# Four dense graph layers, fp32, 64 graphs: row sums by SBUF transfers, products two slots behind the units, and last roots on ScalarE

## The chip, the cores and the metric

One core of a Trainium2 chip runs the whole program. TensorE, VectorE, ScalarE and GpSimd each take their instructions in program order from their own queue, SyncE issues all transfers, and semaphores tie the five together. The metric is the device time of one execution in microseconds (us).

## The reference

There are 64 graphs of 128 nodes with 128 features, all fp32. Each graph goes through four layers, each with a residual and a layer norm.

```python
# layer 0: for all pairs of nodes i, j of a graph
h   = relu((x @ W1[:128])[i] + (x @ W1[128:])[j] + b1)
y   = layernorm(h @ W2 + b2) * gamma + beta
out = sum over j of adj[i, j] * y[i, j]
x   = norm(x + out)
# layer 1: degree-normalised aggregation
x   = norm(x + relu((D^-1/2 adj D^-1/2 x) @ W.T + b))
# layer 2
x   = norm(x + mask * (relu((x + x_agg) @ W1 + b1) @ W2 + b2))
# layer 3: three rounds  h = relu(norm(adj.T @ (h @ Ws[i]) + bs[i] + h) * gamma + beta)
x   = norm(x + h)
```

Layer 0 is nearly all of the work: 16384 pairs a graph, each with a 128x128 product and a norm of its own.

## The kernel before, in words

W2 is centred once (w2c), so that the mean of each pair's y is zero and its norm needs only the mean of squares. For each graph make_uv makes u and v (L402, L403); a unit is one node i: h = relu(v + u[:, i]), 128x128, made by VectorE (L669), ScalarE (L556) or GpSimd (L924). Eight units make a duo, the work of one slot. Sixteen slots make one iteration, and one iteration takes in one new graph. `pool_units` gives GpSimd three units of a slot whose number is in ROOTLESS, and two else; `vector_units` gives VectorE one in every second slot and four in the last; ScalarE makes the rest.

What a slot does is fixed by lags, counted in slots from the start of a graph's iteration:

- Units of duo t at slot t + START (4). They go into a ring `h` of H_RING (18) duos.
- Products y = w2c.T h (L417), TensorE, at t + START + 1, in two blocks of four units, into two PSUM buffers `y_ps`.
- Squares of y (L566), ScalarE, at t + START + 2, ahead of that slot's units.
- Sums of squares (L429, ss_ps), TensorE, once in two slots.
- For each half of a graph (8 duos): standard deviations (L573, Sqrt, ScalarE), four transfers that turn them into `devs`, the inverse (L693) and the coefficients c = adj / deviation (L701) on VectorE, a store to a DRAM scratch, and five transfers that spread c over all partitions into `cb` (L347, L349).
- Weighted sums (L685), VectorE, at t + TTR_LAG (START + 15) for the first four units and one slot later for the others. Each multiplies h by cb in place and adds up along j into a column of gT. They tell by `ttr_done` that a ring buffer is free.

L701 also leaves the row sum of each half row of c in `c_row_sum`. The whole row sum is wanted for b2 (x_base, L744). VectorE copies the halves to rows_sum (L869), two small TensorE products with a matrix row_pick (L450) join and reorder them, and VectorE copies the result to c_sum (L740). `unit_of` interleaves the units, and the load of adj_c follows that order in eight transfers of 32 partitions.

The rest of a graph, its tail, runs two and three iterations after the graph came in, between these. `place(name, slot, fine)` puts each step at a slot and one of nine fine steps in it. Of the norms (NORMS, seven a graph) VectorE makes mean and variance (L709, L712), GpSimd adds eps and raises to the power -0.5 (L912, L915: `var_eps`, `rs`), and VectorE applies them (L718 or L792) seven fine steps after the first. GpSimd also makes the root of the degree (L907).

At the start SyncE loads x, then seven weights (L297); TensorE, VectorE and ScalarE wait for all seven, and TensorE for VectorE's whole set-up of w2c, w2cg, b2cg.

Of the kernel before, what the change touches and what calls it, by code (L numbers as in the profile page):

```python
# [21 lines left out]
TTR_LAG = START + 15  # L22
H_RING = 18
LAYERS = 3
SQ_RING = 4
ROOTLESS = (1, 2, 3, 5, 7, 9, 11, 14)
SPAN = P // 2
WEIGHTS = 7
# [59 lines left out]
for _name, _slot, _fine in [  # L88
    ("adj_turn", 0, 0), ("adj_turned", 0, 6), ("row_sum", 0, 2), ("degree", 0, 5), ("has_degree", 1, 5),
    ("c_sum_mm", 1, 4), ("c_sum", 1, 8), ("x_base", 2, 3),  # L90
# [9 lines left out]
]:  # L100
    place(_name, _slot, _fine)


def build(nc, x, adj, nodemask, l0_W1, l0_b1, l0_W2, l0_b2, l0_gamma, l0_beta, l1_W, l1_b,
# [4 lines left out]
    with ExitStack() as ctx:  # L109
# [6 lines left out]
        def sem(name):  # L116
# [42 lines left out]
        row_pick, rows_sum = sb("row_pick", [P, 2, P]), sb("rows_sum", [P, 2])  # L159
# [26 lines left out]
        c_sum_ps = [prod_bank[b][:, 2, 0:1] for b in range(2)]  # L186

        weights_in, later_weights_in, masks_in = sem("weights_in"), sem("later_weights_in"), sem("masks_in")
# [26 lines left out]
        row_pick_set, rows_kept, c_summed, c_sum_set = (  # L215
            sem("row_pick_set"), sem("rows_kept"), sem("c_summed"), sem("c_sum_set"))
# [60 lines left out]
        def _(sp):  # L277
# [12 lines left out]
            sp.dma_start(x_in[:], x[0]).then_inc(x_in_in, 16)  # L290
            weights = [
                (w1a[:], l0_W1[0:P, :]), (w1b[:], l0_W1[P:2 * P, :]), (b1_col[:], col(l0_b1)),
                (w2[:], l0_W2), (b2_row[:], row(l0_b2)), (b2_col[:], col(l0_b2)), (gamma0[:], row(l0_gamma)),
# [34 lines left out]
            def store_coefficients(g, half):  # L328

                wait_apart(sp, c_made, 2 * g + half + 1)  # L330
                for p in range(CHUNKS):
# [4 lines left out]
                             ).then_inc(c_stored[half], 16)  # L336

# [51 lines left out]
        def _(pe):  # L389
# [44 lines left out]
            def later_layers(g, b, lo, hi):  # L434
# [52 lines left out]
            def later_set_up():  # L487
# [4 lines left out]
                pe.transpose(prod[1][:, 0:G], mask_f[:], ident[0:G, 0:G]).then_inc(mask_turned, 1)  # L492
                pe.wait_ge(wT_set, 1)
# [4 lines left out]
                pe.wait_ge(row_pick_set, 3)  # L498
# [34 lines left out]
        def _(act):  # L533
# [41 lines left out]
            def later_layers(g, b, lo, hi):  # L575
# [37 lines left out]
            act.wait_ge(weights_in, 16 * WEIGHTS)  # L613
            keep_xT(0, 0)
            act.wait_ge(b2c_set, 1)

            def iteration(after, graphs, buf):
                new = graphs[0]
                for s in range(SLOTS):
# [9 lines left out]
                    sg, t = lagging(graphs, s, START + 2)  # L629
# [3 lines left out]
                    vg, t = lagging(graphs, s, START + HALF + 2)  # L633
# [19 lines left out]
                    if s == 13 and after is not None:  # L653
# [6 lines left out]
        def _(dve):  # L660
# [34 lines left out]
            def coefficients(g, half):  # L695

                wait(dve, inv_done, 2 * g + half + 1)
                wait(dve, adj_c_in, 128 * (g + 1))
                wait(dve, c_stored[half], 16 * g)
                wait(dve, rows_kept, g)  # L700
# [3 lines left out]
            def norm_steps(g, b, name, lo, hi):  # L704
# [16 lines left out]
            def later_layers(g, b, lo, hi):  # L721
# [80 lines left out]
            for k in range(PARTS):  # L802
# [13 lines left out]
            dve.wait_ge(b2_meaned, 2)
            dve.tensor_scalar(b2c_col[:], b2_col[:], b2_mean[:], float(P) ** -0.5, ALU.subtract, ALU.mult
                              ).then_inc(b2c_set, 1)
            dve.wait_ge(w2c_set, 1)
            dve.tensor_tensor(w2cg[:], w2c[:], gamma0[:], ALU.mult).then_inc(affine_set, 1)  # L820
            dve.scalar_tensor_tensor(out=b2cg[:], in0=b2_row[:], scalar=b2_mean[:], in1=gamma0[:],
                                     op0=ALU.subtract, op1=ALU.mult).then_inc(affine_set, 1)

            def later_set_up():
# [6 lines left out]
                by_unit = ident[:].rearrange("k (p q n l) -> k q p n l", p=CHUNKS, q=4, l=2)  # L831
# [138 lines left out]
```

## Time and profile before

| what | value |
|---|---|
| median of 3 runs | 2756.13 us (2755.44 to 2756.31) |
| the profiled execution | 2755.1 us, of which the span of its instructions is 2753.5 us |
| busy: PE, DVE, ACT, POOL | 98%, 95%, 93%, 90% of the span |
| mean granted TensorE clock | 0.989 |
| transfers | 571.72 MB, mean 208 GB/s |

PE is TensorE's matmuls, PEld its weight loads, DVE VectorE, ACT ScalarE, POOL GpSimd, SP SyncE; a q behind the name means its sequencer. An fp32 product shows as two matmul records. L12 is line 12 of the kernel. Matmul ends are modelled, so that the starts of two rows say more than the length of one. The chain that ended last names PE for 67% of the span, ACT for 18%, DVE for 8%.

### The profile page before, as it was taken

What the parts mean: (1) busy time and instruction counts of PE and PEld (TensorE: products, weight loads), DVE (VectorE), ACT (ScalarE), POOL (GpSimd) and SP (SyncE); (2) the same over time, 40 slices, a digit from 0 to 9 for tenths busy, and PEclk for the clock granted to TensorE, in tenths of its full rate; (3) what the DMA queues carried; (4) which work ended last, traced back from release to release, by engine and by line L of the source; (5) the groups of instructions that cost most, each with busy time, mean ns of one, the idle gap of its engine ahead of it and who ended that gap; (6) DMA issues with size and microseconds to landing.
All of it is one profiled execution on the core that took longest, in us unless ns stands there. A gap on an engine that the chain in (4) does not pass through costs nothing.

```text
span 2753.5 us, 60836 instructions
## 1 busy us (share of the span) xinstructions
PE 2690.3 (98%) x10882; PEld 1147.3 (42%) x10882; DVE 2619.0 (95%) x20102; ACT 2567.7 (93%) x6903; POOL 2487.8 (90%) x3498
## 2 busy tenths in 40 slices
PE   8999999999999999999999999999999999999993
PEld 2344444444444444444444444444444444444442
DVE  4999999999999999999999999999999999999997
ACT  7999999999999999999999999999999999999991
POOL 3899999999999999999999999999999999999992
PEclk9999999999999999999999999999999999999995
DMA  3655655655555555556556555555655565565562
GB/s 108 237 196 209 231 206 196 231 219 194 215 231 201 202 226 219 197 215 231 199 200 232 214 194 221 227 199 203 230 213 197 214 236 196 202 234 210 195 228 95
DMA packets 188668, 571.72 MB, mean 208 GB/s; under 512 B 70656, under 2 KB 106368, under 8 KB 139136
## 3 DMA queue, kind: packets, MB, share of 16 engines
q1 hardware_dynamic: 188288, 567.83, 54.5%
q14 instruction: 285, 2.33, 0.3%
q8 instruction: 95, 1.56, 0.2%
HBM read 555.17 MB, written 8.39 MB: 205 GB/s over the span
## 4 chain that ended last, share of the span: by engine, by line
PE 67%; ACT 18%; DVE 8%; issue 6%; POOL 1%; DMA 0%; SPq 0%; ACTq 0%; DVEq 0%; POOLq 0%
PE y_ps L417 47%; PE ss_ps L429 13%; ACT h L556 11%; DVE h L685 5%; ACT sq L566 4%; ACT dev_rows L573 2%; PE prod_bank L479 1%; PE prod_bank L483 1%; PE prod_bank L450 1%; ACT hid L595 1%; PE prod_bank L456 1%; PE prod_bank L457 1%; PE uv_ps L402 1%; PE uv_ps L403 1%; POOL h L924 1%
## 5 line engine op out<-in xcount | busy, mean ns | idle before, releaser
L924 POOL TENSOR_SCALAR h<-vT,uT 128x128 f32<-128x128 f32 x2520 | 2056.7, 831 | 23.7 <-ACT vT L546 23.3
L417 PE MATMUL y_ps<-h,w2c 128*128 128x512 f32 x4096 | 2016.4, 609 | 11.4 <-DVE h L669 1.6
L685 DVE CUSTOM_DVE_ANT_0 h<-h,cb 128x128 f32<-128x128 f32 x8192 | 1983.9, 289 | 10.0 <-DVE gT_keep L749 0.5
L556 ACT ACTIVATE h<-uv_ps,uT 128x128 f32<-128x128 f32 x4848 | 1409.2, 433 | 0.0
L566 ACT ACTIVATE sq<-y_ps,b2c_col 128x1024 f32<-128x1024 f32 x1024 | 1182.5, 1155 | 112.3 <-PE y_ps L417 112.1
L417 PEld LDWEIGHTS y_ps<-h,w2c 128*128 128x128 f32 x4096 | 682.2, 190 | 903.6 <-issue 723.7
L685 DVE DVE_READ_ACCUMULATOR2_ANT gT<- 128x1 f32 x8192 | 636.8, 78 | 0.1
L429 PE MATMUL ss_ps<-sq,sel 128*32 128x512 f32 x4096 | 545.5, 605 | 0.9 <-ACT sq L566 0.9
L915 POOL TENSOR_TENSOR rs<-var_eps,minus_half 128x1 f32<-128x1 f32 x448 | 302.7, 676 | 35.1
L669 DVE TENSOR_SCALAR h<-vT,uT 128x128 f32<-128x128 f32 x757 | 200.9, 294 | 4.7 <-ACT mask_all L611 2.6
L912 POOL TENSOR_TENSOR var_eps<-mv,eps_col 128x1 f32<-128x1 f32 x448 | 96.1, 215 | 117.9 <-DVE mv L712 115.0
L429 PEld LDWEIGHTS ss_ps<-sq,sel 128*32 128x32 f32 x4096 | 80.6, 108 | 225.5 <-ACT sq L566 105.0
L709 DVE BATCH_NORM_STATS2 stats<-z 128x6 f32<-128x128 f32 x448 | 127.4, 284 | 0.3
L483 PEld LDWEIGHTS prod_bank<-l3w,aggT 128*128 128x128 f32 x384 | 73.6, 194 | 93.0 <-issue 58.6
L693 DVE RECIPROCAL invs<-devs 128x64 f32<-128x64 f32 x128 | 70.1, 548 | 38.6 <-DMA devs<-dev_rows 35.6
L718 DVE TENSOR_SCALAR x<-z,mv,rs 128x128 f32<-128x128 f32 x256 | 96.7, 378 | 6.2 <-POOL rs L915 4.8
L907 POOL TENSOR_TENSOR dis_raw<-degree_floor,minus_half 128x1 f32<-128x1 f32 x64 | 35.1, 548 | 65.3 <-DVE degree_floor L733 65.3
L599 ACT ACTIVATE aggT<-prod_bank 128x128 f32<-128x128 f32 x192 | 66.3, 345 | 25.3 <-PE prod_bank L479 21.7
L604 ACT ACTIVATE h<-z_aff 128x128 f32<-128x128 f32 x192 | 70.4, 367 | 17.5 <-DVE z_aff L792 17.5
L792 DVE SCALAR_TENSOR_TENSOR z_aff<-z_aff,rs,l3beta 128x128 f32<-128x128 f32 x192 | 81.9, 427 | 4.6 <-POOL rs L915 2.9
L573 ACT ACTIVATE dev_rows<-ss_ps 128x512 f32<-128x512 f32 x128 | 79.8, 624 | 1.2 <-PE ss_ps L429 1.2
L712 DVE BATCH_NORM_AGGREGATE mv<-stats 128x2 f32<-128x6 f32 x448 | 77.8, 174 | 2.6
(100 smaller groups left out, 1489.8 us busy)
## 6 DMA issues: line engine op xcount, KB each, us to landing
cb<-c_scratch SPq DMA_DIRECT2D x384, 1024.0 KB, 9.3
cb<-c_scratch SPq DMA_DIRECT2D x256, 512.0 KB, 4.8
adj_c<-in_adj_dram SPq DMA_DIRECT2D x512, 8.0 KB
devs<-dev_rows SPq DMA_DIRECT2D x512, 8.0 KB
x_in<-in_x_dram SPq DMA_DIRECT2D x64, 64.0 KB, 10.8
c_scratch<-c SPq DMA_DIRECT2D x128, 32.0 KB, 1.5
adj_in<-in_adj_dram SPq DMA_DIRECT2D x64, 64.0 KB, 4.4
x_res<-in_x_dram SPq DMA_DIRECT2D x64, 64.0 KB, 5.4
```

The source lines that it names most:

```text
L417: op = pe.matmul(y_ps[:, t % 2, c0:c0 + COLS], w2c[:], h[:, (SLOTS * g + t) % H_RING, c0:c0 + COLS], start=True, stop=True)
L429: mm = pe.matmul(ss_ps[32 * q:32 * q + 32, :], sel[:, ROWS - 1 - p:ROWS - 1 - p + 32], sq[:, (t + q // 2) % SQ_RING, c0:c0 + COLS], start= ...
L483: pe.matmul(out, aggT[:, b, :], l3w[:, i, :], start=True, stop=False)
L556: op = act.activation(h[:, (SLOTS * g + t) % H_RING, n * P:(n + 1) * P], v, ACT.Relu, bias=uT[:, b, i:i + 1])
L566: act.activation(sq[:, t % SQ_RING, :], y_ps[:, t % 2, :], ACT.Square, bias=b2c_col[:], scale=float(P) ** -0.5).then_inc(sq_done, 1)
L573: act.activation(dev_rows[:, half, :], ss_ps[:], ACT.Sqrt, bias=EPS).then_inc(dev_done, 1)
L669: op = dve.tensor_scalar(h[:, (SLOTS * g + t) % H_RING, n * P:(n + 1) * P], vT[:, b, :], uT[:, b, i:i + 1], 0.0, ALU.add, ALU.max)
L685: op = dve.tensor_tensor_reduce(h[:, (SLOTS * g + t) % H_RING, cols], h[:, (SLOTS * g + t) % H_RING, cols], cb[:, t // 2, c0:c0 + P], 1.0, ...
L709: dve.bn_stats(stats[:, b, :], z[:, b, :]).then_inc(stats_set[name], 1)
L718: dve.tensor_scalar(dst[:, b, :], z[:, b, :], mv[:, b, 0:1], rs[:, b:b + 1], ALU.subtract, ALU.mult).then_inc(normed[name], 1)
L915: pool.tensor_tensor(rs[:, b:b + 1], var_eps[:, b:b + 1], minus_half[:], ALU.pow).then_inc(rs_set[name], 1)
L924: op = pool.tensor_scalar(h[:, (SLOTS * g + t) % H_RING, n * P:(n + 1) * P], vT[:, b, :], uT[:, b, i:i + 1], 0.0, ALU.add, ALU.max)
```

## The change

Eight things are changed together.

1. `unit_of` is the natural order, 8 t + n. adj_c is loaded by two transfers of 128 partitions.
2. The row sums are joined by transfers from SBUF to SBUF (`pair_row_sums`, two a half, 64 elements of 4 bytes each) and one addition on VectorE. rows_sum, row_pick and the two products L450 go.
3. Products, squares, sums of squares, deviations and coefficients come one slot later behind the units (PRODUCT_LAG = START + 2).
4. Weighted sums come one slot later (START + 16), and the ring has 19 buffers. The tail's steps from g_keep on stand one slot later; l0_sum stands two fine steps later behind l0_mm.
5. ROOTLESS is the new list of slots without a root: nine instead of eight, so GpSimd makes one unit more and ScalarE one fewer a graph.
6. W2 is loaded right behind x, then W1 and b1 with a semaphore of their own; b2 and gamma follow. VectorE centres w2 first and does the rest of the set-up after the first slot's units.
7. In the set-up for the later layers TensorE waits two slots later for what it needs of it.
8. For the last graph only, ScalarE takes the square root of variance + eps and VectorE the reciprocal, in place of GpSimd's two operations.

```diff
-TTR_LAG = START + 15
-H_RING = 18
+PRODUCT_LAG = START + 2
+TTR_LAG = START + 16
+H_RING = 19
-ROOTLESS = (1, 2, 3, 5, 7, 9, 11, 14)
+ROOTLESS = (1, 2, 3, 4, 5, 8, 10, 12, 15)
...
 def unit_of(t, n):
-    half, b = t // HALF, 2 * (t % HALF) + n // BLOCK_UNITS
-    return 64 * half + 16 * (b % 4) + 4 * (b // 4) + n % BLOCK_UNITS
+    return DUO_UNITS * t + n
...
-    ("c_sum_mm", 1, 4), ("c_sum", 1, 8), ("x_base", 2, 3),
-    ("g_keep", 3, 4), ("l0_mm", 4, 0), ("l0_sum", 4, 5), ("ln0", 4, 6), ("x1_scaled", 5, 6),
-    ("l1_agg", 6, 0), ("l1_agg_keep", 6, 8), ("l1_mm", 7, 0), ("l1_bias", 7, 7), ("l1_relu", 8, 0),
+    ("c_sum", 1, 8), ("x_base", 2, 3),
+    ("g_keep", 4, 4), ("l0_mm", 5, 0), ("l0_sum", 5, 7), ("ln0", 5, 8), ("x1_scaled", 6, 7),
+    ("l1_agg", 7, 0), ("l1_agg_keep", 7, 8), ("l1_mm", 8, 0), ("l1_bias", 8, 7), ("l1_relu", 9, 0),
...
-                rows = a.rearrange("(h q p n) (l j) -> h p q (n l) j", h=2, q=4, p=CHUNKS, l=2)
+                rows = a.rearrange("(h i) (l j) -> h (i l) j", h=2, l=2)
                 for half in range(2):
-                    for p in range(CHUNKS):
-                        sp.dma_start(adj_c[32 * p:32 * p + 32, half, :], rows[half, p]).then_inc(adj_c_in, 16)
+                    sp.dma_start(adj_c[:, half, :], rows[half]).then_inc(adj_c_in, 16)
...
+            sp.dma_start(w2[:], l0_W2).then_inc(w2_in, 16)
+            first_weights = [(w1a[:], l0_W1[0:P, :]), (w1b[:], l0_W1[P:2 * P, :]), (b1_col[:], col(l0_b1))]
...
+            def pair_row_sums(g, b, half):
+                wait_apart(sp, c_made, 2 * g + half + 1)
+                wait_apart(sp, c_sum_set, g - 1)
+                wait_apart(sp, c_pair_in[half], 32 * g)
+                for l in range(2):
+                    sp.dma_start(c_pair[SPAN * half:SPAN * half + SPAN, b, l:l + 1], c_row_sum[l:P:2, half:half + 1]
+                                 ).then_inc(c_pair_in[half], 16)
...
                     spread_coefficients(old, 0)
+                    pair_row_sums(old, 1 - buf, 0)
...
                     spread_coefficients(old, 1)
+                    pair_row_sums(old, 1 - buf, 1)
...
-                if due("c_sum_mm"):
-                    wait(pe, rows_kept, g + 1)
+                if due("l0_mm"):
                     wait(pe, adjT_set, g + 1)
-                    for half in range(2):
-                        op = pe.matmul(c_sum_ps[b], row_pick[:, half, :], rows_sum[:, half:half + 1],
-                                       start=(half == 0), stop=(half == 1))
-                    op.then_inc(c_summed, 1)
-                if due("l0_mm"):
-                    wait(pe, c_sum_set, g + 1)
...
-                    yg, t = lagging(graphs, s, START + 1)
+                    yg, t = lagging(graphs, s, PRODUCT_LAG)
...
-                    if s == 12 and after is not None:
+                    if s == 13 and after is not None:
                         turn_x(after, 1 - buf)
-                    sg, t = lagging(graphs, s, START + 3)
-                    if s % 2 == 1 and sg is not None:
+                    sg, t = lagging(graphs, s, PRODUCT_LAG + 2)
+                    if t % 2 == 0 and sg is not None:
...
+                for name in NORMS:
+                    if g == G - 1 and lo <= AT[name] + 2 < hi:
+                        wait(act, mv_set[name], g + 1)
+                        act.activation(var_eps[:, b:b + 1], mv[:, b, 1:2], ACT.Sqrt, bias=EPS).then_inc(eps_added[name], 1)
...
-                    sg, t = lagging(graphs, s, START + 2)
+                    sg, t = lagging(graphs, s, PRODUCT_LAG + 1)
...
-                    vg, t = lagging(graphs, s, START + HALF + 2)
+                    vg, t = lagging(graphs, s, PRODUCT_LAG + HALF + 1)
...
+                if g == G - 1 and lo <= at + NORM_AT - 1 < hi:
+                    wait(dve, eps_added[name], g + 1)
+                    dve.reciprocal(rs[:, b:b + 1], var_eps[:, b:b + 1]).then_inc(rs_set[name], 1)
...
-                    wait(dve, c_summed, g + 1)
-                    dve.tensor_copy(c_sum[:, b:b + 1], c_sum_ps[b]).then_inc(c_sum_set, 1)
+                    for half in range(2):
+                        wait(dve, c_pair_in[half], 32 * (g + 1))
+                    dve.tensor_tensor(c_sum[:, b:b + 1], c_pair[:, b, 0:1], c_pair[:, b, 1:2], ALU.add).then_inc(c_sum_set, 1)
...
-            dve.wait_ge(weights_in, 16 * WEIGHTS)
+            dve.wait_ge(w2_in, 16)
...
+                    if is_graph(new, 0) and s == START + 1:
+                        first_set_up()
...
-                    cg, ct = lagging(graphs, s, START + HALF + 3)
+                    cg, ct = lagging(graphs, s, PRODUCT_LAG + HALF + 2)
...
-                        if ct == HALF + 1 and cg is not None and k == FINE - 1:
-                            wait(dve, c_made, 2 * (cg + 1))
-                            wait(dve, c_summed, cg)
-                            dve.tensor_copy(rows_sum[:], c_row_sum[:]).then_inc(rows_kept, 1)
...
-                    if lo <= AT[name] + 1 < hi:
+                    if g < G - 1 and lo <= AT[name] + 1 < hi:
```

## Rows read from the trace of the kernel before

**Rows 1.** The page: busy us (share of the span) and instructions of each engine

```profile
PE 2690.3 (98%) x10882; PEld 1147.3 (42%) x10882; DVE 2619.0 (95%) x20102; ACT 2567.7 (93%) x6903; POOL 2487.8 (90%) x3498
```

**Rows 2.** Windows: stretch, length, busy us of PE, PEld, DVE, ACT, POOL, clock, DMA

```profile
9.40:49.50 40.10, 36.20 (x113) 13.26 (x114) 15.94 (x86) 32.77 (x81) 5.33 (x7) 1.00 0.24 69
171.50:2641.30 2469.80, 2463.16 (x10032) 1051.43 (x10031) 2397.94 (x18468) 2365.21 (x6373) 2317.41 (x3246) 1.00 0.56 213
2641.30:2753.50 112.20, 69.35 (x271) 34.21 (x269) 91.39 (x664) 50.03 (x135) 55.21 (x93) 0.74 0.37 144
```

**Rows 3.** Waits from 1302 to 2138 (twenty graphs): us in total, times, longest

```profile
ACT sq L566 <- PE y_ps L417: 34.2, 80, 0.6
...
POOL var_eps L912 <- DVE mv L712: 21.4, 39, 0.7
...
POOL dis_raw L907 <- DVE degree_floor L733: 18.7, 20, 1.2
DVE z L753 <- PE prod_bank L457: 13.3, 20, 0.8
```

**Rows 4.** Timeline of TensorE in one steady graph: start, length, operation, records

```profile
1307.91 0.22 PE L484 MATMUL prod_bank<-bias_parts,pick 96*128 96x128 bf16 x1
1307.97 1.07 PE L417 MATMUL y_ps<-h,w2c 128*128 128x512 f32 x2
...
1313.10 1.02 PE L417 MATMUL y_ps<-h,w2c 128*128 128x512 f32 x2
1314.05 1.06 PE L429 MATMUL ss_ps<-sq,sel 128*32 128x512 f32 x8
...
1332.80 0.22 PE L484 MATMUL prod_bank<-bias_parts,pick 96*128 96x128 bf16 x1
1333.13 1.98 PE L417 MATMUL y_ps<-h,w2c 128*128 128x512 f32 x4
...
1337.12 2.74 PE L417 MATMUL y_ps<-h,w2c 128*128 128x512 f32 x6
1339.69 0.50 PE L450 MATMUL prod_bank<-rows_sum,row_pick 128*128 128x1 f32 x4
1340.13 1.07 PE L429 MATMUL ss_ps<-sq,sel 128*32 128x512 f32 x8
```

**Rows 5.** The page's groups: GpSimd's units; count, busy us, mean ns, idle before

```profile
L924 POOL TENSOR_SCALAR h<-vT,uT 128x128 f32<-128x128 f32 x2520 | 2056.7, 831 | 23.7 <-ACT vT L546 23.3
```

**Rows 6.** Groups by line of VectorE, 1302 to 2138

```profile
L869 DVE COPY rows_sum<-c_row_sum 128x2 f32<-128x2 f32 x20 | 3.1, 157 | 0.0
```

**Rows 7.** Timeline of SyncE at the start

```profile
2.58 0.43 SPq L297 DMA_DIRECT2D w<-in_L_gnn_W_dram  x1
```

**Rows 8.** Transfers issued from 0 to 12: count, KB each, us to landing

```profile
b_col<-in_L_gnn_b_dram SPq DMA_DIRECT2D x2, 0.5 KB, 2.8
```

**Rows 9.** Timelines of VectorE, TensorE and ScalarE, 0 to 52

```profile
7.73 0.29 DVE L808 TENSOR_REDUCE w_mean<-w 128x1 f32<-128x128 f32 x1 [5.15 <-DMA gamma<-in_L_gnn_gamma_dram]
40.32 0.55 DVE L693 RECIPROCAL invs<-devs 128x64 f32<-128x64 f32 x1 [19.58 <-DMA devs<-dev_rows]
9.38 0.77 PE L402 MATMUL uv_ps<-xT,w1a 128*128 128x128 f32 x2 [6.17 <-DVE b2cg L821]
37.84 1.12 PE L417 MATMUL y_ps<-h,w2c 128*128 128x512 f32 x2 [0.75 <-ACT h L556]
46.87 2.81 PE L417 MATMUL y_ps<-h,w2c 128*128 128x512 f32 x6 [1.45 <-ACT sq L566]
45.49 0.22 ACT L611 ACTIVATE mask_all<-prod_bank 128x64 f32<-128x64 f32 x1
```

**Rows 10.** Timeline near the end: a norm of the last graph

```profile
2733.63 0.18 DVE L712 BATCH_NORM_AGGREGATE mv<-stats 128x2 f32<-128x6 f32 x1
...
2734.74 0.35 DVE L718 TENSOR_SCALAR x<-z,mv,rs 128x128 f32<-128x128 f32 x1 [0.93 <-POOL rs L915]
```

**Rows 11.** L573 alone: operation, count, shortest/median/longest ns, first and last start

```profile
L573 ACT ACTIVATE dev_rows<-ss_ps x128: 597/635/694, 36.2 to 2689.9; 128x512 f32<-128x512 f32 x128
L573 ACT ACT_TABLE_LOAD  x1: 1283/1283/1283, 34.9 to 34.9; - x1
```

More of the change, by code:

```diff
@@ L158, in build @@
         c_row_sum = sb("c_row_sum", [P, 2])
-        row_pick, rows_sum = sb("row_pick", [P, 2, P]), sb("rows_sum", [P, 2])
+        c_pair = sb("c_pair", [P, 2, 2])
         gT, gT_keep = sb("gT", [P, P]), sb("gT_keep", [P, 2, P])
@@ L185, in build @@
         xturn_ps = [prod_bank[b][:, 3, :] for b in range(2)]
-        c_sum_ps = [prod_bank[b][:, 2, 0:1] for b in range(2)]
+        w1_in, w2_in = sem("w1_in"), sem("w2_in")
         weights_in, later_weights_in, masks_in = sem("weights_in"), sem("later_weights_in"), sem("masks_in")
@@ L214, in build @@
             sem("degree_set"), sem("degree_floor_set"), sem("dis_raw_set"), sem("dis_set"))
-        row_pick_set, rows_kept, c_summed, c_sum_set = (
-            sem("row_pick_set"), sem("rows_kept"), sem("c_summed"), sem("c_sum_set"))
+        c_pair_in = [sem(f"c_pair_in{i}") for i in range(2)]
+        c_sum_set = sem("c_sum_set")
         x_base_set = sem("x_base_set")
@@ L284, in load_adj_c_rows @@
             def load_adj_c_rows(a):
-                rows = a.rearrange("(h q p n) (l j) -> h p q (n l) j", h=2, q=4, p=CHUNKS, l=2)
+                rows = a.rearrange("(h i) (l j) -> h (i l) j", h=2, l=2)
                 for half in range(2):
-                    for p in range(CHUNKS):
-                        sp.dma_start(adj_c[32 * p:32 * p + 32, half, :], rows[half, p]).then_inc(adj_c_in, 16)
+                    sp.dma_start(adj_c[:, half, :], rows[half]).then_inc(adj_c_in, 16)
             sp.dma_start(x_in[:], x[0]).then_inc(x_in_in, 16)
+            sp.dma_start(w2[:], l0_W2).then_inc(w2_in, 16)
+            first_weights = [(w1a[:], l0_W1[0:P, :]), (w1b[:], l0_W1[P:2 * P, :]), (b1_col[:], col(l0_b1))]
+            assert len(first_weights) == FIRST_WEIGHTS
+            for dst, src in first_weights:
+                sp.dma_start(dst, src).then_inc(w1_in, 16)
             weights = [
-                (w1a[:], l0_W1[0:P, :]), (w1b[:], l0_W1[P:2 * P, :]), (b1_col[:], col(l0_b1)),
-                (w2[:], l0_W2), (b2_row[:], row(l0_b2)), (b2_col[:], col(l0_b2)), (gamma0[:], row(l0_gamma)),
+                (b2_row[:], row(l0_b2)), (b2_col[:], col(l0_b2)), (gamma0[:], row(l0_gamma)),
             ]
@@ L407, in products @@
                 if block_of_duo == 0:
+                    if g == 0 and t == 0:
+                        pe.wait_ge(w2c_set, 1)
                     if vector_units(g, t) > 0:
@@ L512, in iteration @@
                         later_set_up()
-                    yg, t = lagging(graphs, s, START + 1)
+                    if is_graph(new, 1) and s == LATER_SET_UP_SLOT + 2:
+                        later_set_up_done()
+                    yg, t = lagging(graphs, s, PRODUCT_LAG)
                     if yg is not None:
@@ L562, in squares @@
             def squares(g, t):
+                if g == 0 and t == 0:
+                    act.wait_ge(b2c_set, 1)
                 wait(act, y_done, SLOTS * g + t + 1)
@@ L652, in iteration @@
                         tail_steps(6, 8)
-                    if s == 13 and after is not None:
+                    if s == 14 and after is not None:
                         keep_xT(after, 1 - buf)
@@ L697, in coefficients @@
                 wait(dve, inv_done, 2 * g + half + 1)
-                wait(dve, adj_c_in, 128 * (g + 1))
+                wait(dve, adj_c_in, 32 * (g + 1))
                 wait(dve, c_stored[half], 16 * g)
-                wait(dve, rows_kept, g)
+                wait(dve, c_pair_in[half], 32 * g)
                 dve.tensor_tensor_reduce(c[:, half, :], adj_c[:, half, :], invs[:, half, :], 1.0, 0.0,
@@ L805, in _, with first_set_up @@
                                 ).then_inc(pick_set, 1)
-            dve.wait_ge(weights_in, 16 * WEIGHTS)
+            dve.wait_ge(w2_in, 16)
             dve.tensor_reduce(w2_mean[:], w2[:], AX.X, ALU.add).then_inc(w2_meaned, 1)
-            dve.tensor_reduce(b2_mean[:], b2_row[:], AX.X, ALU.add).then_inc(b2_meaned, 1)
             dve.wait_ge(w2_meaned, 1)
             dve.tensor_scalar(w2_mean[:], w2_mean[:], 1.0 / P, None, ALU.mult).then_inc(w2_meaned, 1)
-            dve.wait_ge(b2_meaned, 1)
-            dve.tensor_scalar(b2_mean[:], b2_mean[:], 1.0 / P, None, ALU.mult).then_inc(b2_meaned, 1)
             dve.wait_ge(w2_meaned, 2)
             dve.tensor_scalar(w2c[:], w2[:], w2_mean[:], None, ALU.subtract).then_inc(w2c_set, 1)
[L816 to L822, printed above, removed]
+            def first_set_up():
+                dve.wait_ge(weights_in, 16 * WEIGHTS)
+                dve.tensor_reduce(b2_mean[:], b2_row[:], AX.X, ALU.add).then_inc(b2_meaned, 1)
+                dve.wait_ge(b2_meaned, 1)
+                dve.tensor_scalar(b2_mean[:], b2_mean[:], 1.0 / P, None, ALU.mult).then_inc(b2_meaned, 1)
+                dve.wait_ge(b2_meaned, 2)
+                dve.tensor_scalar(b2c_col[:], b2_col[:], b2_mean[:], float(P) ** -0.5, ALU.subtract, ALU.mult
+                                  ).then_inc(b2c_set, 1)
+                dve.wait_ge(w2c_set, 1)
+                dve.tensor_tensor(w2cg[:], w2c[:], gamma0[:], ALU.mult).then_inc(affine_set, 1)
+                dve.scalar_tensor_tensor(out=b2cg[:], in0=b2_row[:], scalar=b2_mean[:], in1=gamma0[:],
+                                         op0=ALU.subtract, op1=ALU.mult).then_inc(affine_set, 1)
             def later_set_up():
@@ L830, in later_set_up @@
                 dve.tensor_scalar(ident_eps[:], ident[:], l2eps[:], None, ALU.mult).then_inc(eps_set, 1)
-                by_unit = ident[:].rearrange("k (p q n l) -> k q p n l", p=CHUNKS, q=4, l=2)
-                dve.memset(row_pick[:], 0.0).then_inc(row_pick_set, 1)
-                dve.wait_ge(row_pick_set, 1)
-                for half in range(2):
-                    dve.tensor_tensor(
-                        row_pick[:, half, SPAN * half:SPAN * half + SPAN].rearrange("k (q p n) -> k q p n", q=4, p=CHUNKS),
-                        by_unit[:, :, :, :, 0], by_unit[:, :, :, :, 1], ALU.add).then_inc(row_pick_set, 1)
                 dve.wait_ge(mask_set, 1)
```

15 lines of the change are left out of this document (7 added, 8 removed), and 14 rows, old and new, of the table AT.

## The prediction

> **What bounds the kernel now.** I first read the busy line of the page: all four engines are busy for 90% to 98% of the span [rows 1]. Such a line says only that nothing has much room, not who is the bound. So next come the windows by stage [rows 2]. The starts of L402, once a graph, cut the run into three stages: the first graph, 9.4 to 49.5; a steady stage from 171.5 to 2641.3; and the last 112.2 us. The steady stage is 2469.8 us with 10032 matmul records, 170 a graph, so 59 graphs at 41.86 us. In it TensorE is busy 41.75 us a graph, VectorE 40.64, ScalarE 40.09 and GpSimd 39.28 (each busy time over 59). The granted clock is 1.00 there.
>
> Then the waits of twenty steady graphs [rows 3]. TensorE matmuls have no wait in that list; ScalarE waits for TensorE's y (34.2 / 20 = 1.7 us a graph), VectorE waits for the l0 product (0.67), GpSimd waits for VectorE (21.4 + 18.7 over 20 = 2.0). So three engines wait, in the end, for TensorE. But matmul ends are modelled, so I went to TensorE's timeline of one graph [rows 4] and looked at start-to-start times. Six y records take 1339.69 - 1337.12 = 2.57 us, 0.43 each, with no hole. I find one hole a graph: L484 to the next y is 0.06 us at 1307.91, but 0.33 us at 1332.80, a stall of 0.27. It follows ScalarE's long stretch with the half's square roots, and ends when its units of h are there. TensorE is the bound, with 41.86 - 0.27 = 41.6 us a graph of its own work.
>
> **What the change takes from a steady graph.** (1) The two c_sum products (four records of L450) go. From L450 to the following ss is 1340.13 - 1339.69 = 0.44 us [rows 4]. Without them y is followed by ss directly; two y then ss take 1314.05 - 1313.10 = 0.95 against 0.86 for two y alone, so 0.09 comes back. Net 0.35 us, on TensorE's own path: it counts in full. Bounds: 0.25 (if the reload before ss is dearer here) and 0.44.
> (2) Products go from one slot behind the units to two. ScalarE now makes unit slot t+3, not t+2, between squaring t and t+1, so at the roots of a half TensorE's next y already has its h, and needs only the square before. The 0.27 stall goes; bounds 0 and 0.27. Squares stay directly behind their y, and y has still two PSUM buffers, so that loop gains nothing. Ring 19 with sums 16 slots behind leaves the distance between a buffer's last sum and its next unit unchanged (three slots less one half), and coefficients stay three slots ahead of their sums. The variances move from odd to even slots with their products: no cost.
> TensorE's floor becomes 41.86 - 0.35 - 0.27 = 41.24 us.
>
> **Who is next.** VectorE: busy 40.64, less the rows_sum copy, recorded at 0.157 us [rows 6]; its copy of c_sum becomes an addition of the same size. With under 0.3 of pipeline gaps, 40.8. Its wait for l0 (0.67) shrinks, for l0_sum is two fine steps later behind l0_mm. ScalarE gives one unit to GpSimd and has more slack. GpSimd: nine slots instead of eight with three units, one unit more, 2056.7 / 2520 = 0.82 us [rows 5]. Its idle time is 41.86 - 39.28 = 2.58, of which 2.0 are the waits; the remaining 0.58 sit around its small operations. So it needs 39.28 + 0.82 + 0.58 = 40.68. Both stay under 41.24, by 0.4 and 0.6, if GpSimd's waits of 2.0 shrink to 0.6. I think they do: those are waits of an engine that is early, and the largest, 18.7 / 20 = 0.9 for degree_floor, falls in slot 0, where now the root of the third layer's first norm (0.9 us) stands directly before it. The slots of three units are those without a root. I take 0.02 off for rubbing: 0.60 us a graph. The slow start and end apart, this holds for 61 graphs: **36.6 us**.
>
> **SyncE and the transfers.** The units' natural order makes the adjacency rows two transfers instead of eight, against four tiny ones for row sums. They are queued behind the spread of their half, so no transfer of coefficients waits for them; behind them stand the next x (wanted at slot 13), the second half's deviations (slot 7), adj_c and the tail's loads. Their added wait, c_sum of the graph before, is over by slot 1, before the coefficients of this graph have been stored. The nearest row is b_col, 128 elements of 4 bytes: 2.8 us to landing [rows 8]; their sum is wanted half an iteration later or more. Cost 0; without that cover one landing a graph would sit on VectorE, 2.8 us. The Trainium skill (DMA: Bandwidth & Descriptors, Rules for kernel authors) speaks against this edit: a last dimension that isn't contiguous becomes one descriptor per element, and transfers under 64 KB are mostly overhead. The trace agrees as to the overhead (2.8 us for 0.5 KB); by the page as by the row the sum is the same as long as nobody waits.
>
> **The start.** Now everything waits for gamma: VectorE's first set-up step is at 7.73, TensorE's first uv product at 9.38 [rows 9]. After the change uv needs w1a, w1b and b1, which are issued third to fifth, 0.47 us apart; the fifth issue is at 2.58 [rows 7]. It lands 2.8 later [rows 8], at 5.4; uv starts at 5.6. The other set-up (b2, gamma) moves behind the first units of h; its 1.5 us end before slot 1's units are wanted, since the first y takes over 3 us. Gain **3.8 us**; bounds 3 and 4.2.
> The first graph shows holes of TensorE: 0.75 for ScalarE's h, 1.45 for a square, and VectorE stands 19.58 us before the first deviations, while units for y are behind it in its queue [rows 9]. With one slot more those units are made earlier. I take **1.5 us**, between 0 and 3.
>
> **The end.** For the last graph the seven roots go to ScalarE (Sqrt) and VectorE (reciprocal). From the end of bn_aggr, 2733.81, to x at 2734.74 are 0.93 us [rows 10]. No row has a 128x1 activation; the nearest is 128x64 with 0.22 us [rows 9]. With the reciprocal (a small VectorE operation, 0.157 in rows 6) and two hand-overs of some 0.05, 0.48. It saves 0.45, seven times: **3.0 us**; bounds 0 and 6.5. Nothing else runs on ScalarE there. That sums run a slot later behind the units costs nothing at the end, as they are 14 slots behind the products before and after; if it did, one slot, 2.6.
>
> **The sum.** 36.6 + 3.8 + 1.5 + 3.0 = 44.9. The profiled execution took 2755.1 us (span 2753.5); 2710.2. The median is 1 us above it: **2711 us**.
>
> **Rivals.**
> A (0.58), as above: TensorE stays the bound, 41.18 to 41.42 us a graph, 2701 to 2720.
> B (0.20), GpSimd and VectorE in lockstep: seven times a graph GpSimd waits for VectorE's mv and VectorE then for GpSimd's rs, six fine steps later. With 0.5 us of slack in place of 2.0 a root that comes behind a unit of 0.82 makes VectorE wait. For it: both would be at 99% of the period. Against: VectorE has no wait for rs in rows 3. At 41.42 to 41.85 a graph: 2720 to 2747.
> C (0.07), more than I see: the holes of the first graphs go wholly and the roots save twice as much: under 2701.
> D (0.05), the change doesn't do what it says: the stall only moves and GpSimd eats L450's time; 41.9 a graph with the ends' 8 us partly lost: 2751 to 2761.
> E (0.07), the other side: GpSimd becomes the bound. With 40.68 of work, its waits of 2.0 unshrunk give 42.7, 0.8 above now, times 61: 2755 + 51 - 8 = 2798. It decides from 1.2 us of waits left a graph; 2762 to 2800. For it: these waits are in its queue's order and not only earliness. Against: as B.
> F (0.03), a Sqrt among Relu and Copy makes the last graph reload tables, up to fourteen times 1.28 [rows 11]: 18 us, 2729. Against: 128 Sqrts lie among Squares and Relus in this trace, with one load at the first of them. The Trainium skill (ScalarE: Activation LUTs, What ACT_TABLE_LOAD costs) puts a switch to another set at 2.66 us; by that fourteen would be 37.
>
> **How the numbers follow.** About 0.2% (5.5 us) is what a measurement of this kernel can tell from no change. Faster: A, B, C and F, 0.88. Same: D, 0.05. Slower: E, 0.07. The likeliest's own range is 2701 to 2720. The range for 8 in 10 takes in A, nearly all of B, F and a part of C: 2698 to 2745.
>
> **What would show it.** Right: starts of L402 about 41.26 apart; L484 to y 0.06 everywhere; no wait of 0.67 before L753; uv at 5.6; GpSimd's waits for mv and degree_floor under 1 us a graph; still two table loads; mv to x 0.5 in the last norms. Wrong: VectorE waiting for rs (B), GpSimd 97% busy and TensorE waiting for its h (E), TensorE waiting for squares, or the first transfers landing later than their rows.

## The result and the profile after

The change makes the kernel slower: 2790.45 us median (2788.71 to 2792.69), against 2755.89 before, a ratio of 1.0126 (95% interval 1.0108 to 1.0143). Forecast were 2711 us, and 2698 to 2745 as the range. The profiled execution took 2788.98 us, its span 2787.2.

The page of the changed kernel, its busy line and the head of the chain that ended last:

```profile
PE 2689.5 (96%) x10626; PEld 1099.5 (39%) x10626; DVE 2613.3 (94%) x20042; ACT 2561.6 (92%) x6847; POOL 2562.3 (92%) x3547
...
POOL 67%; DVE 21%; issue 4%; DMA 4%; PE 2%; SPq 2%; ACT 1%; DVEq 0%; POOLq 0%; ACTq 0%
```

TensorE's share has gone from 98% [rows 1] to 96%, and the chain that named PE for 67% of the span names POOL for 67%. So the bound has moved. Next the windows, before and after, cut so that each holds the same 60 graphs (from the uv product of the fourth graph to that of the last), each with the stretch behind it. First the kernel before:

```profile
129.60:2641.30 2511.70, 2504.95 (x10202) 1069.27 (x10201) 2438.52 (x18781) 2405.34 (x6481) 2356.67 (x3301) 1.00 0.56 213
```

Then the changed one:

```profile
120.70:2675.20 2554.50, 2505.83 (x9961) 1023.66 (x9960) 2432.26 (x18721) 2398.28 (x6422) 2431.91 (x3361) 1.00 0.56 209
...
2675.20:2787.20 112.00, 70.78 (x267) 33.88 (x265) 94.26 (x693) 52.21 (x142) 52.23 (x81) 0.73 0.41 154
```

A graph takes 2554.50 / 60 = 42.58 us in place of 41.86. The 60 graphs lose 42.8 us; up to the fourth graph 8.9 are won (129.6 to 120.7), and 0.2 behind the last uv. That is 33.7 in all, the difference of the spans.

Where a graph loses its time is in the waits, here of ten graphs (1910 to 2335) of the changed kernel, total, times and longest:

```profile
ACT sq L581 <- PE y_ps L434: 23.0, 40, 1.1
DVE x L740 <- POOL rs L932: 16.4, 10, 1.7
POOL var_eps L929 <- DVE mv L730: 14.0, 20, 1.0
PEld prod_bank L471 <- DVE x1s L782: 12.6, 10, 1.3
...
PE prod_bank L471 <- DVE x1s L782: 4.4, 10, 0.5
...
PE prod_bank L477 <- DVE x L740: 3.0, 10, 0.3
```

VectorE waits for GpSimd's rs once a graph, 1.64 us, a wait that rows 3 do not have; behind it TensorE waits for x1s and x. In rows 3 nobody waits for GpSimd; now the path leads to it. The timeline of GpSimd shows where:

```profile
2116.44 0.18 POOL L929 TENSOR_TENSOR var_eps<-mv,eps_col 128x1 f32<-128x1 f32 x1
2116.70 0.56 POOL L932 TENSOR_TENSOR rs<-var_eps,minus_half 128x1 f32<-128x1 f32 x1
2117.23 0.64 POOL L924 TENSOR_TENSOR dis_raw<-degree_floor,minus_half 128x1 f32<-128x1 f32 x1
2117.85 14.66 POOL L941 TENSOR_SCALAR h<-vT,uT 128x128 f32<-128x128 f32 x17
2132.49 0.18 POOL L929 TENSOR_TENSOR var_eps<-mv,eps_col 128x1 f32<-128x1 f32 x1
2132.75 0.56 POOL L932 TENSOR_TENSOR rs<-var_eps,minus_half 128x1 f32<-128x1 f32 x1
```

The root of the third layer's first norm and the degree's root stand first, then seventeen units in one run, 14.66 us, then the first norm's root. The same place before the change, from the degree's root on:

```profile
1337.73 0.55 POOL L907 TENSOR_TENSOR dis_raw<-degree_floor,minus_half 128x1 f32<-128x1 f32 x1 [0.92 <-DVE degree_floor L733]
1338.27 10.03 POOL L924 TENSOR_SCALAR h<-vT,uT 128x128 f32<-128x128 f32 x12
1348.88 0.19 POOL L912 TENSOR_TENSOR var_eps<-mv,eps_col 128x1 f32<-128x1 f32 x1 [0.58 <-DVE mv L712]
```

There were twelve units, and GpSimd waited 0.58 us for VectorE. VectorE's side in the same graph as the changed rows above:

```profile
2116.13 0.18 DVE L730 BATCH_NORM_AGGREGATE mv<-stats 128x2 f32<-128x6 f32 x1
...
2130.33 0.17 DVE L730 BATCH_NORM_AGGREGATE mv<-stats 128x2 f32<-128x6 f32 x1
...
2133.35 0.39 DVE L740 TENSOR_SCALAR x<-z,mv,rs 128x128 f32<-128x128 f32 x1 [1.72 <-POOL rs L932]
```

The first norm's mv is there at 2130.50, but GpSimd starts on it only at 2132.49. Both sides of the stretch can be added up from these rows. From 2116.44, where GpSimd starts on the third layer's mv, it waits for nobody until it has made the first norm's rs at 2133.31, 16.9 us later. VectorE wants that rs at 2133.35 - 1.72 = 2131.63, 15.2 us after 2116.44. The difference is the wait.

The new ROOTLESS has slots 1 to 5 in a row, and the first norm's root has moved by eleven fine steps (1.2 slots): five more units stand between it and the degree's. The third layer's first root now falls into slot 0 directly ahead of the degree's, where before GpSimd waited 0.92 us for degree_floor.

### The profile page after: what moved, and what is told of

The parts are those of the page before. It is cut to its first block, busy times and chain, and to the rows that moved or that the text cites. A ratio compares the mean times of both kernels' runs of the same rounds, so it can differ in the third digit from the quotient of the medians.

```text
span 2787.2 us, 60254 instructions
## 1 busy us (share of the span) xinstructions
PE 2689.5 (96%) x10626; PEld 1099.5 (39%) x10626; DVE 2613.3 (94%) x20042; ACT 2561.6 (92%) x6847; POOL 2562.3 (92%) x3547
## 4 chain that ended last, share of the span: by engine, by line
POOL 67%; DVE 21%; issue 4%; DMA 4%; PE 2%; SPq 2%; ACT 1%; DVEq 0%; POOLq 0%; ACTq 0%
POOL h L941 56%; DVE h L703 12%; POOL rs L932 7%; DMA x_res<-in_x_dram 3%; POOL var_eps L929 3%; POOL dis_raw L924 1%; PE y_ps L434 1%; DVE stats L727 1%; DVE invs L711 1%; DVE gT L703 1%; DVE z_aff L815 1%; DVE z_aff L810 1%; DVE z L802 1%; DVE z_aff L785 1%; DVE mv L730 1%
## 5 line engine op out<-in xcount | busy, mean ns | idle before, releaser
L941 POOL TENSOR_SCALAR h<-vT,uT 128x128 f32<-128x128 f32 x2583 | 2161.8, 853 | 18.4 <-ACT vT L559 18.4
L703 DVE DVE_READ_ACCUMULATOR2_ANT gT<- 128x1 f32 x8192 | 627.2, 77 | 0.1
L932 POOL TENSOR_TENSOR rs<-var_eps,minus_half 128x1 f32<-128x1 f32 x441 | 263.0, 596 | 34.6
L929 POOL TENSOR_TENSOR var_eps<-mv,eps_col 128x1 f32<-128x1 f32 x441 | 103.4, 234 | 136.5 <-DVE mv L730 135.5
L740 DVE TENSOR_SCALAR x<-z,mv,rs 128x128 f32<-128x128 f32 x256 | 97.9, 382 | 105.1 <-POOL rs L932 104.6
L493 PE MATMUL prod_bank<-l3w,aggT 128*128 128x128 f32 x384 | 76.6, 282 | 2.6 <-ACT aggT L618 2.6
L815 DVE SCALAR_TENSOR_TENSOR z_aff<-z_aff,rs,l3beta 128x128 f32<-128x128 f32 x192 | 74.7, 389 | 1.7 <-POOL rs L932 1.2
## 6 DMA issues: line engine op xcount, KB each, us to landing
c_pair<-c_row_sum SPq DMA_DIRECT2D x256, 0.2 KB, 10.3
```

The lines of the kernel that those rows point to most:

```text
L493: pe.matmul(out, aggT[:, b, :], l3w[:, i, :], start=True, stop=False)
L703: op = dve.tensor_tensor_reduce(h[:, (SLOTS * g + t) % H_RING, cols], h[:, (SLOTS * g + t) % H_RING, cols], cb[:, t // 2, c0:c0 + P], 1.0, ...
L929: pool.tensor_tensor(var_eps[:, b:b + 1], mv[:, b, 1:2], eps_col[:], ALU.add).then_inc(eps_added[name], 1)
L932: pool.tensor_tensor(rs[:, b:b + 1], var_eps[:, b:b + 1], minus_half[:], ALU.pow).then_inc(rs_set[name], 1)
L941: op = pool.tensor_scalar(h[:, (SLOTS * g + t) % H_RING, n * P:(n + 1) * P], vT[:, b, :], uT[:, b, i:i + 1], 0.0, ALU.add, ALU.max)
```

## The experiments

Theory 1: the run of units ahead of the first norm's root is too long for VectorE's stretch beside it. Theory 2: 41 units a graph are too many, wherever they stand. Theory 3: the tail's loads, wanted in slot 0 as before but issued a slot later behind the spread, come late. The expectations of e1 to e6 count the run too long (21 units for the changed kernel, 19 for e5, 13 for the kernel before); by the order of the program, and in the timelines, it is 17, 15 and 12. "Period" is the median distance of the uv products of neighbouring graphs. e2, e4, e6, e9, e12 and e13 were executed only once each; nine executions of e1 lay between 2746.60 and 2752.29 us, so a single time can be off by a few us.

**Unit taken out of the run, and out of another place.**

```diff
-ROOTLESS = (1, 2, 3, 4, 5, 8, 10, 12, 15)
+ROOTLESS = (1, 2, 3, 4, 8, 10, 12, 15)      # e1
+ROOTLESS = (1, 2, 3, 4, 5, 8, 12, 15)       # e2
```

> The changed kernel with slot 5 taken out of ROOTLESS: GpSimd makes 40 units a graph, as before the change, and the unbroken run of 21 units ahead of the first norm's root becomes one of 20. Theory 1 (the units bunched ahead of that root make VectorE wait for rs, 1.7 us a graph): the wait falls to 0.9 and the period from 42.48 to about 41.7 us, the whole to about 2743. Theory 2 (GpSimd's load of 41 units as such): the same, about 41.65. Theory 3 (loads of the tail that come late because products stand a slot later): period 42.3 to 42.5, about 2785.

> The changed kernel with slot 10 taken out of ROOTLESS instead: also 40 units a graph, but the run of 21 ahead of the first norm's root stays. Theory 1 (bunching): VectorE still waits 1.5 us or more for rs at L740, period 42.2 to 42.5. Theory 2 (load as such): period about 41.65, as with slot 5 taken out. Theory 3 (late tail loads): 42.3 to 42.5, but with no wait for rs.

Measured: e1 2749.57 us, ratio 0.9978 (0.9968 to 0.9987), period 41.82, wait for rs at L740 1.0 us. e2 2782.57 us, period 42.36, wait 1.65. The waits (1910 to 2335), e1 and then e2:

```profile
DVE x L740 <- POOL rs L932: 10.3, 10, 1.0
```

```profile
DVE x L740 <- POOL rs L932: 16.5, 10, 1.7
```

Both have 40 units; the one out of the run is worth 0.66 us a graph, the other 0.12. That speaks for theory 1. In e2 single graphs are up to 1 us longer than the median, beside waits for x_res: theory 3 has a small part.

**Row sums alone, on the kernel before (e3).**

```diff
-    half, b = t // HALF, 2 * (t % HALF) + n // BLOCK_UNITS
-    return 64 * half + 16 * (b % 4) + 4 * (b // 4) + n % BLOCK_UNITS
+    return DUO_UNITS * t + n
...
+                    pair_row_sums(old, 1 - buf, 0)
...
-                if due("c_sum_mm"):
...
-                        op = pe.matmul(c_sum_ps[b], row_pick[:, half, :], rows_sum[:, half:half + 1],
-                                       start=(half == 0), stop=(half == 1))
```

> The kernel before with the row sums by transfers alone (natural unit order, two adj_c transfers, no L450 products), lags, ring, lists, start and roots as they were. The prediction's step: TensorE's path loses 0.35 us a graph, so the period falls from 41.86 to 41.5 and the whole to 2734. Rival (the transfers come too late or the 0.35 is given back as a wait for ScalarE's h): 41.8 to 41.9, within 3 us of before.

Measured: 2745.03 us, ratio 0.9962 (0.9948 to 0.9976), period 41.69. It is a gain, but 0.17 us a graph, not 0.35. The timeline of TensorE in this version:

```profile
2036.55 0.22 PE L485 MATMUL prod_bank<-bias_parts,pick 96*128 96x128 bf16 x1
2036.88 1.98 PE L425 MATMUL y_ps<-h,w2c 128*128 128x512 f32 x4
...
2040.86 2.74 PE L425 MATMUL y_ps<-h,w2c 128*128 128x512 f32 x6
2043.53 1.07 PE L437 MATMUL ss_ps<-sq,sel 128*32 128x512 f32 x8
2044.53 3.01 PE L425 MATMUL y_ps<-h,w2c 128*128 128x512 f32 x6
2047.38 0.38 PE L410 MATMUL uv_ps<-xT,w1a 128*128 128x128 f32 x2
```

y is followed directly by ss (six records 2.67 us, with the 0.09 of the prediction), so the two products did cost what was worked out. The hole of 0.33 behind L485 has stayed, as it must without the lag, and the next six y take 2047.38 - 2044.53 = 2.85 us where the kernel before took 2.68 in the same place:

```profile
1341.12 2.84 PE L417 MATMUL y_ps<-h,w2c 128*128 128x512 f32 x6
1343.80 0.38 PE L402 MATMUL uv_ps<-xT,w1a 128*128 128x128 f32 x2
```

TensorE comes earlier and waits 0.17 us for ScalarE's h: half of the gain was given back to the wait that the lag is for.

**A ninth slot of three units, on the kernel before (e4).**

```diff
-ROOTLESS = (1, 2, 3, 5, 7, 9, 11, 14)
+ROOTLESS = (1, 2, 3, 4, 5, 7, 9, 11, 14)
```

> The kernel before with slot 4 added to ROOTLESS: GpSimd makes 41 units a graph, and the run ahead of the first norm's root grows from 13 units to 14. Theory 1 (bunching): that run had 0.5 and 0.9 us of waiting in it, so one unit of 0.84 is taken in and the period stays at 41.86, within 0.1. Theory 2 (load as such, waits unshrunk): the period grows by up to 0.8, to 42.7.

Measured: 2757.54 us, period 41.85, unchanged. At that period 41 units fit: GpSimd's wait for mv goes from 1.0 us a graph to 0.5 and its idle time takes the unit in.

**The same 40 units spread, and the 41st in two places.**

```diff
-ROOTLESS = (1, 2, 3, 4, 5, 8, 10, 12, 15)
+ROOTLESS = (1, 3, 5, 7, 8, 10, 12, 15)       # e5, 15 ahead of the first norm's root
+ROOTLESS = (1, 3, 5, 7, 8, 10, 11, 12, 15)   # e6
+ROOTLESS = (1, 3, 5, 7, 8, 10, 12, 14, 15)   # e12
```

> The changed kernel with ROOTLESS = (1, 3, 5, 7, 8, 10, 12, 15): 40 units for GpSimd, 19 in the run ahead of the first norm's root in place of 21, one of the moved units right behind that root, where GpSimd waited 1.0 us for mv. Theory 1 (bunching): VectorE's wait for rs falls from 1.7 us to under 0.3, the period to TensorE's floor of about 41.2, at most 41.4; the whole 2712 to 2722. Theory 2 (load as such): 41.8, as with slot 5 taken out. Theory 3 (late tail loads as a second bound): up to 41.6 on the mean, with single periods up to 1 us longer than the median.

> As the one before with slot 11 added: 41 units, as many as the changed kernel has, but still 19 in the run ahead of the first norm's root. Theory 1: under 0.3 us above the 40-unit version's period, 41.2 to 41.6. Theory 2 (load as such): 42.4, as the changed kernel.

> The 40-unit spread version with slot 14 added in place of slot 11: 41 units, 15 ahead of the first norm's root, the extra one ahead of ln3's root, whose run has only 2. If it is the place of a unit that decides (six ahead of one root with slot 11), the period is 41.2 to 41.4. If it is the number 41, 41.8 or more wherever it stands.

Measured: e5 2708.55 us, ratio 0.9823 (0.9809 to 0.9838), period 41.19. Against the changed kernel's list one of GpSimd's units has moved (out of slots 1 to 5, into slot 7) and one is dropped; that turns 1.3% slower into 1.8% faster. Its window of 60 graphs:

```profile
121.30:2596.70 2475.40, 2473.82 (x9962) 1033.41 (x9961) 2437.91 (x18723) 2394.28 (x6481) 2375.68 (x3302) 1.00 0.58 216
```

TensorE is busy 2473.82 of 2475.40 us: it is the bound again, and VectorE waits 0.1 us a graph for rs. But the 41-unit versions take 2747.27 us with a period of 41.86 (e6), and 2739.72 with 41.70 (e12). Neither theory had these periods (41.2 to 41.6 or 42.4 for e6). I had expected the place to decide; it decides 0.16, and the 41st unit costs at least 0.5 a graph even where only three stand ahead of a root. In e6 the wait is at the root behind the six units:

```profile
DVE z_aff L815 <- POOL rs L932: 7.7, 10, 0.8
```

In e12 VectorE waits at two roots a graph:

```profile
DVE x L740 <- POOL rs L932: 8.2, 20, 0.6
```

So theory 2 has a part too, once the run is short.

**Fewer units, spread and bunched.**

```diff
-ROOTLESS = (1, 2, 3, 4, 5, 8, 10, 12, 15)
+ROOTLESS = (1, 3, 5, 8, 10, 12, 15)          # e9
+ROOTLESS = (1, 2, 3, 4, 5, 10, 12)           # e13
```

> The changed kernel with ROOTLESS = (1, 3, 5, 8, 10, 12, 15): 39 units for GpSimd, one more for ScalarE. (The runs of units are counted here by program order: between the degree's root and the first norm's root the changed kernel has 17, not 21 as the expectations before said; this version has 15.) If TensorE's own work is the floor at 41.19, one unit less on GpSimd changes nothing: 41.19, within 0.05. Rival (GpSimd still takes part in the bound): 41.0 or less. Second rival (ScalarE, with one unit more, becomes late): above 41.3 and TensorE waits for h.

> ROOTLESS = (1, 2, 3, 4, 5, 10, 12): only 39 units a graph, two fewer than the changed kernel and one fewer than before the change, but the run of 17 ahead of the first norm's root kept whole. Theory 1 (bunching ahead of that root): VectorE's wait at L740 stays above 1 us and the period at 42.0 or more. Theory 2 (load as such): 41.19, as GpSimd then has 1.7 us less to do than in the changed kernel.

Measured: e9 2708.53 us, period 41.19: one unit less than the spread 40 changes nothing, so GpSimd is no longer in the bound there. e13 2787.9 us, period 42.46, with two units less than the changed kernel and within 3 us of its time. e9 and e13 have the same number of units on every engine and differ only in the slots; the place alone is worth 79 us. Its window and its waits (1910 to 2335), to be read beside those of the changed kernel above:

```profile
121.20:2674.10 2552.90, 2505.58 (x9962) 1023.11 (x9961) 2429.26 (x18721) 2421.44 (x6541) 2344.96 (x3241) 1.00 0.56 209
```

```profile
POOL var_eps L929 <- DVE mv L730: 28.8, 30, 1.4
...
DVE x L740 <- POOL rs L932: 17.2, 10, 1.7
```

GpSimd is busy 39.1 us of 42.55 and waits 2.9 for mv, and still VectorE waits 1.7 for it. That is the clearest result of the study: the two units saved turned into waits of GpSimd, because ahead of the one root the run of 17 is as long as before and everywhere else it is VectorE, late from that root, that sets the pace.

**The tail's loads ahead of the spread (e7).** On e5:

```diff
                     store_coefficients(old, 1)
+                    load_tail(old, 1 - buf)
                     spread_coefficients(old, 1)
...
-                    load_tail(old, 1 - buf)
```

> The 40-unit spread version, and SyncE issues the two loads of the tail (adj_in, x_res) between the store of the second half's coefficients and their spread, not behind the spread, the row sums and adj_c. Theory 3 (tail loads land after VectorE and TensorE want them in slot 0): no more waits for x_res at the transpose of adj_in, no single periods longer than the median, 0.1 to 0.2 us a graph less on the mean. Rival (they were no bound): the same within 0.05, or the spread is late by it and VectorE waits for cb.

Measured: 2706.46 us, ratio 0.9817 (0.9803 to 0.9832), the fastest version. The waits for x_res are gone and the mean period falls from 41.26 to 41.23; the 2 us between the two versions are within the intervals. Some single periods are still longer than the median, so not all of these were the loads'. In the changed kernel TensorE and VectorE waited for them like this, over the whole run:

```profile
  PEld prod_bank L462: 22.3, 29
  DVE degree L751: 7.6, 10
  PE prod_bank L462: 6.4, 10
```

**The lags taken out (e8).** The row-sum version with the new start and the last roots on ScalarE, but products one slot behind the units. The table of places, with l0_sum's two fine steps, goes back to the old one too:

```diff
-PRODUCT_LAG = START + 2
-TTR_LAG = START + 16
-H_RING = 19
+TTR_LAG = START + 15
+H_RING = 18
-ROOTLESS = (1, 2, 3, 4, 5, 8, 10, 12, 15)
+ROOTLESS = (1, 2, 3, 5, 7, 9, 11, 14)
```

> The row-sum version of the kernel before, with the new order of the start and the last roots on ScalarE, but products, squares and sums at the old lags, ring 18 and the old ROOTLESS: the changed kernel without its lags. Expected: the period of the row-sum version, 41.69, unchanged; uv of the first graph at 4.7 in place of 9.4, and 3.1 us less behind the last g_keep; together 2745 - 4.7 - 3.1 - about 1 = 2736. If the slot more is worth what the prediction said, the spread 40-unit version lies another 0.3 to 0.5 us a graph below it, 20 to 25 us in all; if it is worth nothing, both are the same within 3 us.

Measured: 2742.20 us, ratio 0.9946 (0.9930 to 0.9963), 6 us more than expected. Its ends win 6.5 us of the 8.8 expected against the row-sum version (3.9 up to the fourth uv, 2.6 behind the last), and the period, 41.75, is 0.06 longer, which takes 3.8 back: the hole behind the bias product is 0.35 and the six y at the place shown above take 2.89. Why is open. Against e5, with the same 40 units, the slot more is worth 41.75 - 41.19 = 0.56 us a graph, some 34 us, more than the 0.3 to 0.5 expected: the stall of 0.27, the 0.17 that the row sums had given back, and 0.12 that is not accounted for. ROOTLESS and the table of places differ between the two as well, and no run takes them apart.

**The last roots back on GpSimd (e10).** On e7, the edits of the last graph's roots undone:

```diff
-                    if g == G - 1 and lo <= AT[name] + 2 < hi:
...
-                    if g < G - 1 and lo <= AT[name] + 1 < hi:
+                    if lo <= AT[name] + 1 < hi:
```

> The 40-unit spread version with the tail's loads first, and the last graph's roots back on GpSimd. Expected from the traces: 3.1 us more behind the last g_keep (33.0 in place of 29.9), nothing else; 2709.5 in place of 2706.5. Rival: the roots are hidden and the time is the same within 1 us.

Measured: 2708.71 us, ratio 0.9832 (0.9819 to 0.9846), 2.2 us more than e7, while its trace has 32.8 us behind the last g_keep against 29.9. Sign and size agree with the predicted 3.0; the intervals of the two versions overlap, so it is the traces that show it.

## Why the prediction was wrong

**The step that failed** is in "Who is next": GpSimd stays under TensorE's floor "if GpSimd's waits of 2.0 shrink to 0.6. I think they do", with the reason that "the slots of three units are those without a root". GpSimd's work was priced nearly right: predicted 40.1 busy, measured 2431.91 / 60 = 40.5, in part as the units of the long run take 14.66 / 17 = 0.86 us each and not 0.82. The wait for degree_floor, 0.9 a graph, went as predicted. But the wait for mv did not shrink: it grew from 21.4 / 20 = 1.1 to 14.0 / 10 = 1.4, and 40.5 + 0.58 + 1.4 = 42.5 is the measured period. Such a sum closes for any engine and shows no cause; the cause is shown by e9 and e13. Nor are slots without a root a safe place: the fastest list has slot 7, where a root stands, and lacks slots 2 and 4.

The limit is between two hand-overs: from the degree's root to the first norm's root GpSimd has 17 units where it had 12, and VectorE's stretch beside them did not grow by as much. To see it I should have counted the units between neighbouring roots, which needs only ROOTLESS, the table of places and 0.84 us a unit: five more are 4.2 us, for a root that moved by 1.2 slots of 2.6 us, 3.2. Less the 0.58 us of waiting there before, that is 0.4 of wait for rs, the right kind and too small a size; measured were 1.64. In the changed kernel the third layer's root, 0.8 us with its var_eps, belongs to the stretch too, since GpSimd no longer waits between it and the degree's. And the longer run takes 14.66 - 10.03 = 4.6 us more and not 4.2. That makes 0.4 + 0.8 + 0.4 = 1.6.

**The rivals.** B named the mechanism (VectorE waits for rs, the two engines in lockstep) but ended it at 41.85, without a reason other than the period before. E had the price (2762 to 2800 holds the measured time), with the right point of decision: 1.2 us of waits left, and 1.4 were; but its sign, TensorE waiting for GpSimd's h, did not come. It was given 0.07. "Against: VectorE has no wait for rs in rows 3" was the weak argument: those rows were taken with another spread of the units.

**The terms.** One by one they came out as follows; the first row and the last are from traces, the first graphs' is what is left over.

| term | predicted | measured |
|---|---|---|
| floor of a graph on TensorE | 41.24 us | 41.19 (e5, e7, e9) |
| 61 graphs | -36.6 us | +42.8 (60 graphs) |
| first uv product | -3.8 us | -4.7 |
| first graphs | -1.5 us | -1.4, not clean |
| last roots | -3.0 us | -3.1 in the trace |

For the first graphs: 8.9 us are won up to the fourth uv, less 4.7 for the start is 4.2. But uv now stands one slot earlier against the products, which comes back behind the last uv; there 0.2 are won though the roots alone give 3.1. So 4.2 - 2.9 = 1.3 to 1.4 remain. The same sum for e5 gives 2.5 (8.3 up to the fourth uv and 2.0 behind the last, less 4.7 and 3.1), so that it is no clean measure of the first graphs. For the start, the row [rows 8] was read wrongly: its 2.8 is the median of two transfers, and in the kernel before they took 2.1 and 3.4. b1 is the first of them:

```profile
2.58 0.44 SPq L295 DMA_DIRECT2D b_col<-in_L_gnn_b_dram  x1
...
4.72 0.80 PE L417 MATMUL uv_ps<-xT,w1a 128*128 128x128 f32 x2 [1.66 <-DMA b_col<-in_L_gnn_b_dram]
```

That is 2.1 us from issue to use, not 2.8. For the roots, a norm of the last graph:

```profile
2769.74 0.18 DVE L730 BATCH_NORM_AGGREGATE mv<-stats 128x2 f32<-128x6 f32 x1
2769.96 0.20 ACT L599 ACTIVATE var_eps<-mv 128x1 f32<-128x1 f32 x1 [1.73 <-DVE mv L730]
2770.19 0.17 DVE L733 RECIPROCAL rs<-var_eps 128x1 f32<-128x1 f32 x1 [0.27 <-ACT var_eps L599]
2770.39 0.34 DVE L740 TENSOR_SCALAR x<-z,mv,rs 128x128 f32<-128x128 f32 x1
```

From mv's end at 2769.92 to x are 0.47 us, against 0.93 [rows 10] and a predicted 0.48; the changed kernel's trace still has two table loads (rival F).

**The lag.** The hole goes with it: in the changed kernel and in e5 the bias product is followed by y after 0.06 us everywhere, and the wait of 0.67 for l0 is gone. That the two gains were not independent was missed: the 0.35 of the row sums is had in full only with the lag (0.17 without it).

**The transfers.** Nobody waited for c_pair, as predicted. Missed was another: the lag moves the second half's coefficients, and so the tail's loads behind them, one slot later, while their first use stays in slot 0, and x_res was late in some graphs. It also took 9.0 us to land in place of 5.4, but that comes with the row sums and not with the lag: it took 8.9 in e3 and e8 as well, where it was late only once, as before the change. It explains the single longer periods only in part; the mean of the changed kernel lies 0.1 us a graph above its median, about 6 us in all at most.

What stays open is why the 41st unit costs 0.5 to 0.7 us a graph at the faster period, more than GpSimd's sum of 40.7 against 41.19 lets expect, and why its place decides only 0.16 of it.

## What to carry to other kernels

Where two engines hand over to each other several times in a period, give each stretch between two hand-overs its own sum on both sides; a total that leaves room says nothing about the fullest stretch. When steps are shifted against work that stays in its slots, count again what stands between them, the transfers too. And take a bundle apart before judging it: here one list of slots, with one unit more in it, cost 82 us and hid a gain of 47.

## What the runs showed of the hardware that I had not expected

A transfer of 0.2 KB issued behind the spread of coefficients took 10.3 us to land (median), though 0.5 KB took 2.1 us among the first loads of the program. That its time is that of the transfers ahead of it is shown by the two loads of the tail: x_res, 64 KB, took 9.0 us in the changed kernel, issued behind the spread, and 2.0 us in e7, issued ahead of it. The changed kernel's rows, then e7's:

```profile
c_pair<-c_row_sum SPq DMA_DIRECT2D x256, 0.2 KB, 10.3
...
x_res<-in_x_dram SPq DMA_DIRECT2D x64, 64.0 KB, 9.0
```

```profile
x_res<-in_x_dram SPq DMA_DIRECT2D x64, 64.0 KB, 2.0
```

The same GpSimd operation on 128x128 takes 0.78 to 0.82 us in pairs (1.55 to 1.64 for two), 0.80 to 0.85 in runs of five (4.02 to 4.24) and 0.86 in the long run of the changed kernel. Why is open; whether it depends on what VectorE does beside it was not tried.
